# Attention scores as three fp32r products in a fused attention and mixture-of-experts kernel, with GpSimd's group order rewritten

## The reference

```python
x = x + attention(layernorm(x), W_qkv, W_out, s)     # x: (4, 512, 256), float32
x = x + experts(layernorm(x), gating_w, w1, b1, w2, b2)

# attention: 32 query heads, 8 key/value heads, head width 64
proj = x @ W_qkv                       # q (32 heads), k (8), v (8)
q, k = rope(q), rope(k)                # x1*cos + x2*sin, -x1*sin + x2*cos
attn = einsum('bqhmd,bkhd->bhmqk', q, k) / 8
attn = where((q_pos >= k_pos) & (q_pos < k_pos + 64), -inf, attn)
w = softmax(concat([attn, sink]))[..., :-1]
out = einsum('bhmqk,bkhd->bqhmd', w, v) @ W_out

# experts: 8 experts, top 2, capacity ceil(tokens*2/8*1.25), hidden width 1024
buf[e, slot] = x                       # scatter by the routing
h = relu(buf @ w1 + b1); out_e = h @ w2 + b2
out[token] += weight * out_e           # gather, weigh, add
```

## Time and profile before

| | us |
|---|---|
| median of 3 runs | 1070.59 (1068.76 to 1070.92) |
| the profiled execution | 1065.58 |
| its span | 1063.8 |
| PE busy | 1032.3 (97%) |
| DVE busy | 918.9 (86%) |
| POOL busy | 663.4 (62%) |
| ACT busy | 653.7 (61%) |

### The profile page before, as it was taken

The page is one execution under the profiler, slowest core; times in us unless marked ns, Lnnn a source line. Parts: engine busy times, 40 slices in busy tenths (PEclk is TensorE's granted clock), DMA queues, the critical chain, the costliest instruction groups (busy, mean ns, idle before and its releaser), DMA issues.

```text
span 1063.8 us, 32339 instructions
## 1 busy us (share of the span) xinstructions
PE 1032.3 (97%) x13013; PEld 729.8 (69%) x13013; DVE 918.9 (86%) x1962; ACT 653.7 (61%) x1670; POOL 663.4 (62%) x607
## 2 busy tenths in 40 slices
PE   6899999999999999999999999999998999999996
PEld 4466666666666666666666666666566999999995
DVE  6999999999999999999999999999966777677773
ACT  4676667666667666667776656777654455544451
POOL 5657776767666888666777877667762422233332
PEclk8999999999999999999999999999999999999998
DMA  3544555544333344333343344333324344454421
GB/s 94 150 114 117 129 135 130 137 118 131 95 84 81 95 110 105 97 100 79 80 111 101 95 131 111 94 86 98 100 80 159 87 121 121 126 125 124 101 44 21
DMA packets 115574, 112.11 MB, mean 105 GB/s; under 512 B 35264, under 2 KB 103936, under 8 KB 115296
## 3 DMA queue, kind: packets, MB, share of 16 engines
q1 hardware_dynamic: 97648, 90.29, 31.3%
q0 software_dynamic: 7296, 8.55, 5.0%
q10 hardware_dynamic: 10480, 11.20, 3.8%
HBM read 74.84 MB, written 21.83 MB: 91 GB/s over the span
## 4 chain that ended last, share of the span: by engine, by line
PE 60%; DVE 35%; issue 2%; ACT 1%; DMA 0%; SPq 0%; POOLq 0%; DVEq 0%
PE bank L1536 21%; DVE probs_ring L1124 15%; DVE probs_t L1133 13%; PE bank L1701 11%; PE bank L1512 11%; PE bank L1712 7%; DVE heads_sb L1153 4%; PE bank L1715 4%; PE bank L1568 1%; PE bank L1441 1%; PE bank L1676 1%; PE bank L1458 1%; PE bank L1476 1%; PE bank L1596 1%; DVE neg_max L1124 0%
## 5 line engine op out<-in xcount | busy, mean ns | idle before, releaser
L841 ACT ACTIVATE probs_ring<-probs_ring,neg_max 128x512 f32<-128x512 f32 x512 | 365.9, 717 | 210.2 <-DVE neg_max L1124 209.4
L1124 DVE CUSTOM_DVE_ANT_0 probs_ring<-bank,mask,sink_neg 128x512 f32<-128x512 f32 x512 | 360.3, 738 | 24.9 <-PE bank L1512 23.8
L1133 DVE STREAM_TRANSPOSE probs_t<-probs_ring 128x1024 f32<-128x1024 f32 x256 | 317.8, 1241 | 0.2 <-ACT probs_ring L841 0.2
L1512 PE MATMUL bank<-qk_st 64*128 64x512 f32 x1024 | 280.6, 624 | 11.6 <-DVE neg_max L1124 7.4
L1536 PE MATMUL bank<-probs_t,v_quads 32*64 32x256 f32 x8192 | 247.9, 381 | 0.0
L1536 PEld LDWEIGHTS bank<-probs_t,v_quads 32*64 32x64 f32 x8192 | 179.3, 132 | 75.4 <-issue 48.1
L670 POOL TENSOR_TENSOR chunk_sb<-chunk_sb,rope_sb 128x512 f32<-128x512 f32 (+1 forms) x94 | 119.8, 1275 | 111.1 <-issue 80.6
L789 POOL DMA_INDIRECT out<-expert_sb,slots x40 | 77.8, 1945 | 150.6 <-DVE expert_sb L1385 143.3
L1512 PEld LDWEIGHTS bank<-qk_st 64*128 64x128 f32 x1024 | 85.3, 185 | 77.0 <-DVE neg_max L1124 41.5
L1043 ACT ACTIVATE hidden<-bank,b_sb 128x320 f32<-128x320 f32 x128 | 60.5, 524 | 107.1 <-PE bank L1701 107.1
L675 POOL TENSOR_TENSOR qk_st<-chunk_sb,swap_sb 128x512 f32<-128x512 f32 (+1 forms) x94 | 120.0, 1276 | 7.4
(11 more groups left out here) (189 smaller groups left out, 1352.5 us busy)
## 6 DMA issues: line engine op xcount, KB each, us to landing
v_quads<-v_rows SPq DMA_DIRECT2D x128, 128.0 KB
recip_wide<-recip_rows SPq DMA_DIRECT2D x64, 256.0 KB
w_raw<-in_L_ffn_w SPq DMA_DIRECT2D x14, 1024.0 KB, 8.2
swap_sb<-chunk_sb SPq DMA_DIRECT2D x314, 32.0 KB
w_raw<-in_L_attn_W_qkv SPq DMA_DIRECT2D x32, 256.0 KB, 2.9
slots<-slot_rows SPq DMA_DIRECT2D x9, 662.5 KB, 4.0
...
```

Of the source, the lines that this page charges most:

```text
L841: nc.scalar.activation(probs[(g * UNITS + n) % RING][:, :], probs[(g * UNITS + n) % RING][:, :], ACT.Exp, bias=neg_max[j][:, n:n + 1], sca ...
L1124: nc.vector.tensor_tensor_reduce(probs[(g * UNITS + n) % RING][:, :], SCORE[SCORE_OF[n // 2][n % 2]][:, :], mask[:, L - P - t * P:2 * L - ...
L1133: nc.vector.transpose(probs_t[j][:, :, (h // 2) * (2 * P):(h // 2 + 1) * (2 * P)] .rearrange("p b (h q) -> p h b q", h=2)[:, :, :, t * BLK ...
L1512: nc.tensor.matmul(SCORE[SCORE_OF[n // 2][hh]][:, :], qk_st[j][half, h // 2, t * P:(t + 1) * P], qk_st[j][half, PAIRS, :], start=True, sto ...
```

## The change

- **Scores.** `qk_st` goes. For `k`, Q01 and Q23 there is now a high part (`k_hi`, `q01_hi`, `q23_hi`, fp32r) and a low part (`k_lo`, `q01_lo`, `q23_lo`). A pair of units is three products by two row halves: q_hi k_hi, q_lo k_hi, q_hi k_lo.
- **Parts.** GpSimd adds the rotated halves in place into `chunk_sb`, ACT rounds that to the high part (`high_part`), and GpSimd subtracts it to give the low part (`low_part`). In the first group DVE makes the low parts of KV and Q01.
- **GpSimd's order.** `rotate` is cut into `turn_parts`, `sum_parts` and `low_part` with positions of their own. The high part of the next weights is made by ACT; `w_raw` has one buffer from the third group on. The two additions to `x_sb` stand at separate positions, and the scatters at r = 92, 99, 108, 115 and 124.
- **SP's order.** The swap of KV comes ahead of `recip_spread`; `k` is copied twice, as high and as low part; the load of weights comes behind `v_in`.
- **Routing.** `x2T` is now a view of `xn2`. GpSimd clears an empty row in it in position 12 of the first period, and `zero_rows` sends that. The slot numbers (`IDS_AT`) are written later, and the high parts of the first expert's `w2` come at positions 9 and 11 of the last group.

```diff
-        ROT_AT = {2: Q23, -12: KV, -11: Q01}
-        SPLIT_AT, SECOND_SPLIT_AT = -15, -10
+        TURNED_AT = {1: Q23, -10: KV, -9: Q01}
+        SUM_AT = {2: Q23, -10: KV, -7: Q01}
+        HIGH_AT = {2: Q23, -8: KV, -6: Q01}
+        LOW_AT = {4: Q23, -8: KV, -5: Q01}
+        W_HIGH_AT, W_LOW_AT = -15, -13
...
-        SCATTER_AT = {89: (0, 1), 99: (2,), 105: (3, 4), 115: (5,), 121: (6, 7)}
+        SCATTER_AT = {92: (0, 1), 99: (2,), 108: (3, 4), 115: (5,), 124: (6, 7)}
...
+            def sum_parts(g, c):
+                q, rows = g * CHUNKS + c, rows_of(c)
+                pool.wait_ge(s_pool, before_group + (q - Q23 + 1) * ROT_STEPS)
...
-                nc.gpsimd.tensor_tensor(qk_st[j][rows, PAIRS if c == KV else c - Q01, :], straight, swapped,
+                nc.gpsimd.tensor_tensor(chunk_sb[c][rows, :], chunk_sb[c][rows, :], swap_sb[c][rows, :],
                                         ALU.add).then_inc(s_rot, 1)
+            def low_part(g, j, c):
...
+                pool.wait_ge(s_qk_hi, q + 1)
...
+                nc.gpsimd.tensor_tensor(low_of(c, g)[rows, :], chunk_sb[c][rows, :],
+                                        high_of(c, j)[rows, :].bitcast(F32), ALU.subtract).then_inc(s_qk_lo, 1)
...
+            def high_part(g, j, c):
...
+                act.wait_ge(s_rot, q + 1)
...
+                nc.scalar.activation(high_of(c, j)[rows, :], turned[rows, :], ACT.Copy).then_inc(s_qk_hi, 1)
...
+                if n == W_HIGH_AT and 0 < g < GROUPS - 1:
+                    act.wait_ge(s_w_in[0], (g + 1) * 48)
+                    act.wait_ge(s_proj, g * CHUNKS)
+                    nc.scalar.activation(w_hi[1 - j][:, :, :], w_raw[0][:, :, :], ACT.Copy).then_inc(s_w_hi, 1)
...
                     if n == UNITS // 2:
-                        pe.wait_ge(s_rot, g * CHUNKS + Q23 + 1)
+                        pe.wait_ge(s_qk_lo, g * CHUNKS + Q23 + 1)
...
-                    for hh in range(2):
-                        half = slice(hh * HD, (hh + 1) * HD)
-                        nc.tensor.matmul(SCORE[SCORE_OF[n // 2][hh]][:, :], qk_st[j][half, h // 2, t * P:(t + 1) * P],
-                                         qk_st[j][half, PAIRS, :], start=True, stop=True).then_inc(s_scores, 1)
+                    c = Q01 + h // 2
+                    for m, (q, k) in enumerate([(high_of(c, j), k_hi[j]), (low_of(c, g), k_hi[j]), (high_of(c, j), k_lo[j])]):
+                        for hh in range(2):
+                            half = slice(hh * HD, (hh + 1) * HD)
+                            ins = nc.tensor.matmul(SCORE[SCORE_OF[n // 2][hh]][:, :], q[half, t * P:(t + 1) * P],
+                                                   k[half, :], start=(m == 0), stop=(m == 2))
```

196 lines of the change are left out of this document (126 added, 70 removed).

## The result

The changed kernel takes **1171.77 us** (median of four runs), the kernel before 1070.03 beside it; by the means of the runs it is 1.093 times as long (95% interval 1.086 to 1.099), and so are the later ratios. The forecast was 1120 with a range of 1082 to 1145. The sign held, and so did the closed path that the forecast rests on; but the growth was twice the forecast, the result lies outside the range, and a good part of it comes from costs that the forecast had put at nothing.

A forecast was written before the change was run, and what follows sets the result against it. The prediction took a closed path over GpSimd, SP and the swap's landing to bound the changed kernel; +5 + 12 + 27 + 7 - 3 + 1.5 = +49.5, rounded 50, on 1070.6 gave 1120 us, range 1082 to 1145.

The forecast's parts named there:

- The saving on PE: Score pairs on PE: three fp32r passes instead of an fp32 pair save 0.17 us a pair, swallowed by GpSimd's slower path.
- Rival 4: Score passes on PE are no cheaper as fp32r: a pair takes 1.29 us, +110 us; chance 0.02.
- The circle: Closed path per group over GpSimd's list, SP's queue and the Q23 swap's landing: 24.2 us a group, +5 us.
- Rival 1 and 2: 1: GpSimd and SP keep up, 1054 us, chance 0.12. 2: only scatters cost, path at most 23.5, 1082 us, chance 0.11.
- small operations: GpSimd's rows of seven (1.7 us, three times) and six (1.2 us, twice) small operations: +7 us.
- The scatters: Six periods with a scatter between Q23's sum and low part: GpSimd waits 3.45 us plus 1.03 for the scatter, +27 us.
- The rule against the change: DVE and GpSimd port sharing in SBUF: L1124 reads scores from PSUM, so added GpSimd work costs DVE nothing.
- Zero rows: Eight periods after a zero-row transfer: the Q23 swap lands 1.5 us later each, +12 us.
- The end at nothing: Routing's shared buffer, later slot numbers and `w2`'s parts cost nothing, since their readers come a period or more later.
- The first group: DVE makes two low parts of 0.7 us in the first group and waits for ACT between: +1.5 us.
- Rival 3: ACT's high parts delay exponentials, so DVE's transpose comes 1 us later in every group: 31 us more, 1151; chance 0.09.

The follow-up runs named there:

- e3: Changed kernel with only the high-part product in the scores, as fp32r; stretch from first to last reciprocal 824.9 us against 835.3.
- e4: Changed kernel with one true fp32 product of the high parts replacing the three score products; stretch from first to last reciprocal 832.9 us against 835.3.
- e1: Changed kernel plus one unused 1.28 us GpSimd product a period at position 4; stretch from first to last reciprocal 857.5 us against 835.3.
- e2: Changed kernel plus one unused 1.28 us GpSimd product a period at position 12; stretch from first to last reciprocal 843.8 us against 835.3.
- e13: Changed kernel with SP's load of weights moved up behind the swap of Q01; stretch from first to last reciprocal 812.0 us against 835.3.
- e7: Changed kernel with DVE's small routing operations moved to positions 14 and 15 of the period before; stretch from first to last reciprocal 829.4 us against 835.3.
- e5: Changed kernel with each transfer of zero rows at position 2 instead of 13; stretch from first to last reciprocal 820.5 us against 835.3.
- e16: Changed kernel with all eight zero-row transfers at positions 2 to 9 of one period; stretch from first to last reciprocal 831.6 us against 835.3.
- e14: Changed kernel with zero rows at position 2, single scatters at 10, DVE's small operations moved earlier, load of weights moved up; 1094.66 us, 1.027 times the kernel before.
- e12: Kernel before with DVE's small routing operations moved from positions 5 and 6 to 2 and 3; 1082.83 us against 1075.1 on the same chip.
- e8: Changed kernel with SP's swap of Q23 ahead of the load of weights, low weights behind Q23's low part; stretch 849.3 us against 835.3.

## Why the prediction was right or wrong

For the groups the terms add up to +48 and +89.8 us came. The 41.8 that are missing stand almost wholly in periods 2 to 9 (33.5 for 12) and in periods 13, 21 and 29 (21.6 for nothing). Outside the groups +4.1 came for +1.5, and +12.5 for nothing.

- **The saving on PE: right and swallowed.** 0.16 us a pair against 0.17 forecast, at three of the four places compared, and e3 and e4 show that it counts for next to nothing here. Rival 4 is out.
- **The circle: right.** 24.5 in the mean of eleven against 24.2. e1, e2 and e13 show that list, SP and landing make it. Rival 1 and 2 fall with it. The other 14 periods grew by 6.7 us, for which the sum had some 2 of its +5 and the +7 for small operations. GpSimd's seven are in its list as forecast (17.4 us against 15.7 in periods 12, 20 and 28).
- **The scatters: the right wait, and the sum met by luck.** +28.0 in the six periods for 27, but five of them carried it and not six; the page's waits have 28.7 us of GpSimd for `recip_wide`. The six waits average 4.8 us, not 3.45; period 31, behind which no group is prepared, did not pay. Too small a wait times one period too many came out even; the five grew by 5.4 us each, for 4.5. The start of the turn that this term counted from has no row; it is this one of the kernel before:

```profile
384.69 1.29 POOL L670 TENSOR_TENSOR chunk_sb<-chunk_sb,rope_sb 128x512 f32<-128x512 f32 x1
```

- **The rule against the change: this step failed, and it cost some 16 to 21 of the 41.8 us missing in the groups.** I read L1124 alone, saw that its scores come from PSUM, and let the added GpSimd work cost DVE nothing. The rule is about operations with two inputs in SBUF, and the routing of a batch has eight of them, each 0.16 to 0.19 us before. The step should have asked which lines of DVE read two tiles of SBUF and where they stand against GpSimd's new list. At positions 5 and 6 of periods 13, 21 and 29 GpSimd idled before and works after. e7 takes 20.5 us from these periods, 15.7 net. The operations themselves grew by 15.2 us, on DVE's own path; in periods 13 and 21 GpSimd also waited 4.5 and 4.0 us for a `k_hi` behind late exponentials.
- **Zero rows: the term was about right, and this step failed beside it: the other costs of its periods were put at nothing.** 12 forecast, 12 to 15 by e5 and e16. But periods 2 to 9 grew by 33.5. I had priced landing alone (1.0 us more where I took 1.5), not SP's issue (4.00 us for 2.45) or its wait for `v_rows`, and these periods also hold the loads of `w_out` and the late normalisation. Some 10 us go when the load of weights leaves the circle (e13, e14), and 9.7 stay open.
- **The end at nothing: failed.** +12.5. The old rows landed late for PE: 3.38 us of waiting and slower passes behind it, 6.2 us together. The scatters at r = 124 come three positions later than those at 121 did; the last starts 5.7 us ahead of the last reciprocal, before 10.7. No run moves them back, so this cause is read from the traces. I had taken the later scatters as free because their readers come a period later. This reader did not. Some 5 us more are ACT's stop, which is no part of the change (last section): e12, of the kind of before but with the stop, takes 276.0 us there for 271.2.
- **The first group**: +4.1 for +1.5. It is 50 to 53.5 in all kernels of the changed kind; it was not taken apart.
- **Rival 3** (ACT's waits add up in every group) did not come in ordinary periods; in periods 3 and 6 GpSimd waited 1.7 us for `k_hi`, and e8 shows that it is near, once the low weights don't cover ACT.
- **Slips in the sum.** 3 x 1.7 + 2 x 1.2 is 7.5 and not 7, and the low ends of the terms give 1099 and not 1097. Neither matters here.
